# Reordering TensorE and VectorE work inside the graph loop of a fused GNN and mixture-of-experts kernel

## The reference

```python
# graph layer, on x = layernorm(x)
h      = relu(bn(conv1d(x, conv1_w, k=1)))
x_conv = relu(bn(conv1d(h, conv2_w, k=17)) + x)
s      = x @ w_se.T + b_se                      # 3 columns
A      = exp(-dist(s)) * adj
x_nmp  = A @ relu(x @ w_msg.T + b_msg)
gi     = [x_conv, x_nmp] @ w_ih.T + b_ih        # r, z, n
gh     = x @ w_hh.T + b_hh                      # r, z, n
r, z   = sigmoid(gi_r + gh_r), sigmoid(gi_z + gh_z)
n      = tanh(gi_n + r * gh_n)
x1     = x_in + (1 - z) * n + z * x
# expert layer, on xn = layernorm(x1) * gamma + beta
logits = xn @ Wr + br; top 2 of 8, softmax weights
y      = sum over the two experts of (gelu(xn @ W1[e] + b1[e]) @ W2[e] + b2[e]) * w[e]
out    = x1 + y
```

## Time and profile before

| what | value |
|---|---|
| median of 3 runs | 616.95 us |
| the profiled execution, its own time | 613.4 us |
| its span, first to last instruction | 611.6 us |
| granted TensorE clock, mean | 0.992 of full speed |
| busy share: PE, PEld, DVE, ACT, POOL | 96%, 84%, 78%, 60%, 56% |

### The profile page before, as it was taken

One profiled execution on the slowest core, in us unless ns is written; L12 is line 12 of the kernel. 1 busy time (PEld: TensorE's weight loads), 2 busy tenths in 40 slices (PEclk: granted clock), 3 DMA queues, 4 the chain that ended last, 5 costly groups with the idle time before them and its releaser, 6 DMA issues. The chain is left out here.

```text
span 611.6 us, 12890 instructions
## 1 busy us (share of the span) xinstructions
PE 587.0 (96%) x3936; PEld 515.5 (84%) x3936; DVE 478.4 (78%) x2014; ACT 366.6 (60%) x733; POOL 339.5 (56%) x249
## 2 busy tenths in 40 slices
PE   8999999999999999999999999999999999999991
PEld 6887778786879797979898989898898979999890
DVE  7978888898788988898989797979787966644330
ACT  5644637365858484848485767666675745655540
POOL 2000505133367577777776767778686563555765
PEclk9999999999999999999999999999999999999996
DMA  8519171725466757566666656657556778666853
GB/s 298 200 65 331 48 258 57 241 66 177 122 191 145 194 128 207 127 177 156 173 163 155 159 162 157 182 140 187 146 153 148 214 163 239 139 154 134 224 96 43
DMA packets 85861, 99.72 MB, mean 163 GB/s; under 512 B 7521, under 2 KB 62561, under 8 KB 85473
## 3 DMA queue, kind: packets, MB, share of 16 engines
q1 hardware_dynamic: 64064, 82.37, 43.3%
q0 software_dynamic: 21728, 16.53, 16.8%
HBM read 74.95 MB, written 30.39 MB: 172 GB/s over the span
## 5 line engine op out<-in xcount | busy, mean ns | idle before, releaser
L1013 POOL DMA_INDIRECT out<-y_t,xt x88 | 160.4, 1823 | 85.4 <-DMA out<-y_t,xt 53.0
L1048 POOL DMA_INDIRECT routed<-row,at_u x112 | 116.9, 1043 | 140.4 <-DVE at_u L1255 109.0
L570 PE MATMUL C<-cv_h,w_hi 128*128 128x256 f32 (+1 forms) x432 | 129.1, 299 | 3.3 <-ACT tz L926 1.5
L571 PE MATMUL C<-cv_l,w_hi 128*128 128x256 f32 (+1 forms) x432 | 123.4, 286 | 0.0
L572 PE MATMUL C<-cv_h,w_lo 128*128 128x256 f32 (+1 forms) x432 | 123.3, 286 | 0.0
L570 PEld LDWEIGHTS C<-cv_h,w_hi 128*128 128x128 f32 x432 | 81.7, 189 | 7.2 <-issue 3.2
L571 PEld LDWEIGHTS C<-cv_l,w_hi 128*128 128x128 f32 x432 | 81.5, 189 | 0.9
L572 PEld LDWEIGHTS C<-cv_h,w_lo 128*128 128x128 f32 x432 | 81.5, 189 | 0.7
L749 PE MATMUL G<-ex,msg_t 128*128 128x512 f32 x128 | 58.2, 597 | 1.7 <-ACT gh L945 1.7
L651 PE MATMUL Y<-w_t,ge 128*128 128x128 f32 x424 | 55.8, 274 | 0.0
L651 PEld LDWEIGHTS Y<-w_t,ge 128*128 128x128 f32 x424 | 51.7, 191 | 3.1 <-issue 2.6
(11 more groups left out here) (273 smaller groups left out, 1614.3 us busy)
## 6 DMA issues: line engine op xcount, KB each, us to landing
w_t<-w_all SPq DMA_DIRECT2D x63, 392.0 KB, 3.6
adj<-adj_t SPq DMA_DIRECT2D x16, 1024.0 KB, 5.8
xt<-routed SPq DMA_DIRECT2D x63, 144.0 KB, 2.4
wd<-w_all SPq DMA_DIRECT2D x11, 392.0 KB, 5.2
x_ln<-x SPq DMA_DIRECT2D x16, 256.0 KB, 2.8
x_res<-x_t SPq DMA_DIRECT2D x16, 256.0 KB, 6.0
out<-x SPq DMA_DIRECT2D x15, 256.0 KB, 3.9
w_all<-w_s SPq DMA_DIRECT2D x1, 3136.0 KB, 9.7
```

Of the source, the lines that this page charges most:

```text
L570: pe.matmul(psum, hi(w), rhs_h, start=start, stop=False)
L571: pe.matmul(psum, hi(w), rhs_l, start=False, stop=False)
L1013: nc.gpsimd.indirect_dma_start(out=out, out_offset=bass.IndirectOffsetOnAxis(ap=xt[j][:, t, R_ID:R_ID + 1].bitcast(U32), axis=0), in_=y_t[ ...
L1048: nc.gpsimd.indirect_dma_start(out=routed, out_offset=bass.IndirectOffsetOnAxis(ap=ats_u[d % 2][:, n:n + 1], axis=0), in_=rows[d % 2][:, n ...
```

## The change

It makes four edits. On TensorE the whole of `conv_sum` now comes ahead of `states`; the candidate's product with the input (hn) comes ahead of those of z and r in graphs 0 to 14 (`d < ROUTED`, so not in graph 15, where as in graph 15 before it waits for `xnT_f32`); the bias products are issued two at a time at four places of graph 1 and four of graph 2, VectorE's sum of them and SyncE's store of `w_all` move to graph 3, TensorE's wait for `b1_set` goes, and the stores of the padding rows move from graphs 2 and 3 to graphs 1 and 2. On VectorE the gate sum and `tile_split(4)` come ahead of the half sum.

```diff
 # SyncE
-                if g == 1:
+                if g == 3:
                     sp.wait_ge(w12_ready, 2)
                     sp.wait_ge(w2_loaded, 16)
                     sp.wait_ge(b1_set, 1)
...
+                if g == 1:
+                    sp.dma_start(routed[DUMMY + TAKEN:, :], pads[TAKEN:, :]).then_inc(pads_stored, 16)
                 if g == 2:
-                    sp.dma_start(routed[DUMMY + TAKEN:, :], pads[TAKEN:, :]).then_inc(pads_stored, 16)
-                if g == 3:
                     sp.dma_start(out[TOKENS + TAKEN:, :], pads[TAKEN:, 0:P]).then_inc(pads_stored, 16)
 # TensorE
-                    for n in range(16):
-                        last = pe.matmul(H0[:, n:n + 1], w1_raw[:, n * P:(n + 1) * P], vec[:, V_BETA:V_BETA + 1],
-                                         start=True, stop=True)
-                    last.then_inc(pe_b1, 1)
+
+                def bias_products(first):
+
+                    if is_graph(g, 1) or is_graph(g, 2):
+                        for n in range(first + 2 * (g - 1), first + 2 * g):
+                            last = pe.matmul(H0[:, n:n + 1], w1_raw[:, n * P:(n + 1) * P], vec[:, V_BETA:V_BETA + 1],
+                                             start=True, stop=True)
+                        last.then_inc(pe_b1, 1)
+
                 tile_a(0)
+                bias_products(0)
...
-                conv_sum(0, 5)
+                conv_sum(0, TAPS_A)
                 if tail:
                     pe.wait_ge(x1T_ready, d + 1)
                     pe.wait_ge(s_f32, g + 1)
                     states(STATES)
-                conv_sum(5, TAPS_A)
                 tile_b(0)
+                bias_products(4)
...
-                if is_graph(g, 1):
-                    pe.wait_ge(b1_set, 1)
...
                 tile_b(1)
+                bias_products(8)
                 conv_diff(14, TAPS)
...
+                if d < ROUTED:
+                    product_hn()
                 product(G1[:], HH + 1, xlT_h[:], xlT_l[:], stop=False)
                 product(G2[:], HH, xlT_h[:], xlT_l[:], stop=False)
-                if tail and d >= ROUTED:
+                if d >= ROUTED:
                     pe.wait_ge(xnT_f32, d - ROUTED + 1)
-                product(G0[:], HH + 2, xlT_h[:], xlT_l[:]).then_inc(pe_hn, 1)
+                    product_hn()
+                bias_products(12)
                 if more:
                     pe.wait_ge(xl_ready, g + 2)
 # VectorE
-                    dve.wait_ge(pe_b1, 1)
+                if is_graph(g, 3):
+                    dve.wait_ge(pe_b1, 8)
...
                 tile_weigh(2)
+                dve.wait_ge(pe_n, g + 1)
+                dve.wait_ge(gate_step, 2 * g + 1)
+                nc.vector.tensor_tensor(tr[:], tr[:], C2[:], ALU.add).then_inc(gate_step, 1)
+                tile_split(4)
                 dve.wait_ge(gru_step, 2 * g + 1)
                 dve.wait_ge(x_res_loaded, 16 * g + 16)
                 nc.vector.scalar_tensor_tensor(out=gr[:], in0=gr[:], scalar=0.5, in1=x_res[:], op0=ALU.mult,
                                                op1=ALU.add).then_inc(x1T_half, 1)
-                dve.wait_ge(pe_n, g + 1)
-                dve.wait_ge(gate_step, 2 * g + 1)
-                nc.vector.tensor_tensor(tr[:], tr[:], C2[:], ALU.add).then_inc(gate_step, 1)
-                tile_split(4)
                 tile_own(3)
```

More of the change, by code:

```diff
@@ L736, in iteration, with product_hn @@
                 pe.wait_ge(exp_done, NT * g + NT)
+                def product_hn():
+                    product(G0[:], HH + 2, xlT_h[:], xlT_l[:]).then_inc(pe_hn, 1)
+                if d < ROUTED:
+                    product_hn()
                 product(G1[:], HH + 1, xlT_h[:], xlT_l[:], stop=False)
                 product(G2[:], HH, xlT_h[:], xlT_l[:], stop=False)
-                if tail and d >= ROUTED:
+                if d >= ROUTED:
                     pe.wait_ge(xnT_f32, d - ROUTED + 1)
-                product(G0[:], HH + 2, xlT_h[:], xlT_l[:]).then_inc(pe_hn, 1)
+                    product_hn()
+                bias_products(12)
                 if more:
```

## The result

The changed kernel took 624.88 us (median; 623.32 to 625.45), the kernel before 617.42 us beside it on the same chip: **1.1% slower, ratio 1.0111 [1.0081, 1.014]**. The forecast was 614.5 us, in a range of 612.4 to 617.4. It was wrong in sign and in size.

A forecast was written before the change was run, and what follows sets the result against it. TensorE was taken to bound tiled graphs, ScalarE's and VectorE's chains the untiled ones. Shifts of -2.72 us through graph 4, -0.40 at graph 5 and +0.7 in graphs 6 to 15 gave -2.4: 614.5 us, range 612.4 to 617.4.

The forecast's parts named there:

- Gate sum first: VectorE's gate sum ahead of the half sum: 0.60 us gained per untiled graph, 0.40 at graph 5's head, nothing in tiled graphs.
- Candidate's product first: `gh` ready earlier, so the message product does not wait: 0.59 us kept in graph 0, 0.15 in graph 3.
- States behind the sum: On TensorE, a new 0.07 us wait for `both` in graphs 6 to 15, +0.7 us; no cost in graphs 3 and 4.
- rival 2: ScalarE's state copies run in series, tap 0.36 us late: tiled graphs +3.6, graphs 1 to 4 +1.2; 618.6 us; chance 0.11.
- Bias products: Spread over graphs 1 and 2: VectorE 2.07 us earlier in graph 1 with other gains; 0.70 us lost in graph 2.
- Should it be late by the same 0.88: Graph 3's `x_ln` load beside the moved `w_all` store: 0.6 us covered by VectorE's idle time; counted zero, at most +0.3.
- the copies follow as they did, at no cost: Graphs 3 and 4: moved states end at 73.21 in graph 2's times, before `xlT` ends, so ScalarE's copies lose nothing.
- the sum's terms for graphs 2, 3 and 4: Shifts added per graph against the profiled execution: +0.70, -0.75 and -0.60 us, reaching -2.72 at graph 4's end.
- the marks I had set: Wrong if tiled graphs differ over 0.2 us, graph 2 isn't longer than graph 3, or last adds' start and end part.

The follow-up runs named there:

- e5: The changed kernel again, nothing edited: 612.51 us against 614.94 for the kernel before, ratio 0.9964.
- e8: The kernel before with only the gate sum moved ahead of the half sum: 612.77 us, ratio 0.9962.
- g1: The kernel before itself, run for its trace: 614.56 us, ratio 0.9994.
- e7: The kernel before with only the candidate's product moved ahead of z and r: 613.89 us, ratio 0.999.
- m2: The kernel before with candidate's product first, gate sum first, and GpSimd's row stores of graphs 0 to 2 held back: 612.45 us, ratio 0.996.
- e2: The kernel before with only the states moved behind the ninth tap: 615.07 us, ratio 1.0006.
- e3: The changed kernel with bias products, `w_all` store and padding stores back where they were: 611.54 us, ratio 0.995.
- e6: The kernel before with only the bias products, `w_all` store and padding stores moved: 616.28 us, ratio 1.0023.
- e4: The changed kernel with GpSimd's row stores of graphs 0 to 2 held until the next graph's `both`: 611.9 us, ratio 0.9953.
- g2: The changed kernel with GpSimd's row stores of graphs 0 to 2 held until the next graph's `both`, run once more: 612.98 us, ratio 0.997.
- m1: The kernel before itself, run for its trace on another occasion: 614.67 us, ratio 0.9995.
- f1: The changed kernel, third time, nothing edited: 625.89 us against 618.39 for the kernel before, ratio 1.0132.
- f2: The kernel before with only candidate's product first and gate sum first: 622.32 us, ratio 1.007.
- k1: The changed kernel with row stores of graphs 0 to 2 held and `w_all` stored behind graph 3's loads: 610.2 us against 615.73, ratio 0.9917.
- f4: The changed kernel with `w_all` stored behind graph 3's loads and states back between taps 5 and 6: 623.07 us, ratio 1.0084.
- e1: The changed kernel with states back between taps 5 and 6: 611.35 us against 614.58 for the kernel before, ratio 0.9956.

## Why the prediction was wrong

There are two answers, since the changed kernel has two times.

**Without late signals (e5)** it is 2.43 us faster by the medians (614.94 to 612.51); the forecast said -2.4 us. That agreement is partly luck:
- *Gate sum first*: forecast -0.60 a graph for graphs 1 to 4 and -0.40 at graph 5, -2.8 in all; e8 measured -2.2 by the medians, and -2.6 at graph 5 against g1, which has the same stretch at half the clock in graph 1. Right in kind.
- *Candidate's product first*: forecast -1.0 in all; e7 shows -1.19 at graph 5, of which 0.69 in graph 0 (forecast 0.59). Right by the trace; the medians (-1.05) do not tell it from nothing. Whether it adds in full to the gate sum, m2 does not settle.
- *States behind the sum*: forecast 0.07 us a tiled graph. The shift of e5 goes from -1.42 to -1.06 over graphs 5 to 14, 0.04 a graph, and e2 shows the same. No wait for `tz` in a tiled graph of e5 from graph 6 on: rival 2's copies in series did not happen. In graph 1 the moved states cost some 0.5 us while the bias products stand in one block (e2 against g1: +1.84 against +1.42 at graph 1; e3's longest wait for `tz` is 0.8 us too); the changed kernel does not have that.
- *Bias products*: graph 1, forecast -2.7 at its gate sum, measured -2.79. Graph 2, forecast a loss of 0.70, measured 0.42 between the gate sums.
- **The step that failed here**, on the store of `w_all` in graph 3, is "Should it be late by the same 0.88, 0.6 of that is covered by VectorE's idle time ...; I count zero, at most +0.3". VectorE waited 3.07, which cost 1.9 us in e5, and 3.8 us in e6 together with a stretch at half the clock. I carried the price of the earlier trace rows from graph 1 to graph 3. The store's lead is indeed the same 7.5 us (45.29 to 52.76 before, 96.84 to 104.34 in e5), and VectorE comes 3.8 us behind the load's issue in both (56.60; 108.19). But the load took 4.7 us in graph 1 and 6.9 in graph 3, where GpSimd's row stores had run until 100.81 and the state's store was issued at 99.11; with the row stores held (e4, g2) it took 6.0, so 0.9 of the 2.2 us goes with them, and the other 1.3 is open.
- The missing 1.9 us hardly shows in the medians, because the kernel before is 1.4 us longer in other executions than in the one the forecast was made against (its graph 1 in the traces of g1 and m1, behind the block of bias products, at half the clock), and no trace of the changed kernel, which has no such block, has that. This is a gain of the bias edit for which the forecast had no term: it priced the products by their records and took the clock behind them as full.
- The base was mixed as well: the trace is one without late signals (613.4 us), the median of 616.95 is 2 us above what the kernel before takes on the occasions without them (614.5 to 614.9). The forecast of 614.5 us was therefore 2 us over the 612.51 of e5, though the change was right.

**With late signals (the result on record, f1)** it is 7.5 us slower. The step that failed is "In graphs 3 and 4 ... the copies follow as they did, at no cost", and the sum's terms for graphs 2, 3 and 4: +0.70, -0.75 and -0.60 forecast, +1.94, +5.49 and +4.70 measured between the gate sums. Not the place of the states is wrong in it but its base: it took for granted that a result is known when it is there, since the one trace I had showed so. No rival had this cause. Rival 2 had the sign and the place (ScalarE's copies, then `both`), but its price of 0.3 us a graph came from the copies and not from what releases them, and it was looked for in the tiled graphs, which lose little (+9.06 to +11.79 over nine).

Of the marks I had set, two say it: graph 2 (28.8 us between gate sums) is not longer than graph 3 (32.3; in e5 it is not either, 27.3 and 28.7), and the last add of the earlier trace rows starts at 530.44 where it had 518.55, 11.9 us later, with the end of the span 11.3 later. The start and the end did move together.

**Shown:** the loss comes and goes with the occasion (1.0111, 1.0132 against 0.9964, same program). Where it comes, TensorE's signals are late in graphs 2 to 4, in the second half of a run of GpSimd's row stores, and in graphs 3 and 4 they are released just after it. It needs neither the states' new place nor the bias edit (f2). With the stores held, the held graphs have no late signal in a trace that has some elsewhere (k1). **Not shown:** the same on one chip side by side, since k1 met late signals in another set than f1 to f4; and how the stores would hold a signal, since the held stores ran beside other signals of TensorE in k1 without making them late. **Open:** why the kernel before, with the same stores, loses only 1 to 4 us on such occasions (615.7, 617.4 and 618.4 against 614.5 to 614.9); two attempts to trace it there met none. Open too is what sets such an occasion off.

## What to carry to other kernels

A gain found in one trace is a gain under that trace's conditions: where an edit moves a chain of one engine's results, another's copies and the first's next step against a run of indirect DMAs of GpSimd, measure it on several chips and occasions before believing either sign. A run of small indirect stores that nobody needs soon can be held until the chain that does matter is through; one wait did it here, at no measurable cost (e4 and g2: 0.9953 and 0.997, e5: 0.9964). And a big store does not cost its own time but the lateness of the small load behind it: issue the load first, and look at when the reader arrives in the very graph to which the store moves. And compare traces of one kernel before one of them is made the base: here a single stretch at half the clock made 1.4 us between two of them.

## What the runs showed that I had not expected

- The same program on two occasions differs by 2.2% (612.5 and 625.9 us) while the kernel before differs by 0.6% (614.9 and 618.4). The chip is not the cause by itself: one chip gave late signals with k1 and none with m1 and m2.
- TensorE's semaphore events, 0.01 us behind the matmul's end in every case without the effect, came up to 4.9 us behind it.
- Traces with late signals also lack records of DMA completions: 4,667 to 4,939 of them in after, f1 to f4 and k1, against 7,335 to 7,378 in the other traces. Semaphore events of the engines are missing too: 2,344 to 2,391 against 2,835 to 2,848. The profile's list of DMAs shows the first of these: from 200 to 500 us the loads `w_t<-w_all` (KB each, median us to landing) have a landing in e5, the first row, and none in k1, the second:

```profile
w_t<-w_all SPq DMA_DIRECT2D x38, 392.0 KB, 4.0
```

```profile
w_t<-w_all SPq DMA_DIRECT2D x38, 392.0 KB
```

Lost records and late signals together let one suspect the recording of events itself, which would then be part of the measured time. No run here separates the two. The Trainium skill's page NOTIFIC — the notification-queue block, section 7.1 (Overflow: three behaviours, one of which stalls the engine), says that this block's inner pipeline holds its producers back rather than lose a record, and section 2.2 (What "attached to" means) counts the event and semaphore unit among the producers. That would fit the late signals and not the lost records, and no run here shows it.
- TensorE's clock fell to half within or just behind a 4 us wait and stayed there 3.4 to 6.8 us, so graphs 2 to 4 lost 12.1 us with waits that sum to 10.3 (1.90, 4.18 and 4.18). Behind shorter waits it is not the same each time: e1, e5 and e6 all wait 1.40 us for the router's products (`pre`) in graph 3, and the clock fell in e1 and e6 and not in e5.
